# Block order of the second and third count products in a four-layer graph network on one Trainium2 core

## The reference, cut to what matters

```python
deg_inv_sqrt = jnp.where(deg > 0, jax.lax.rsqrt(jnp.maximum(deg, 1.0)), 0.0)
w = deg_inv_sqrt[src] * deg_inv_sqrt[dst]
x = emb
out = emb
for _ in range(NUM_LAYERS):              # 3
    x = jax.ops.segment_sum(w[:, None] * x[src], dst, num_segments=n)
    out = out + x
return out / (NUM_LAYERS + 1)
```

## Time and profile before

| | |
|---|---|
| median of 3 runs | 1010.4 us (1008.99 to 1014.34) |
| the profiled execution's own time | 1007.57 us |
| its span in the trace | 1005.9 us |
| TensorE matmul busy | 840.9 us (84%), 14240 instructions |
| VectorE busy | 856.4 us (85%), 1214 instructions |
| ScalarE busy | 616.1 us (61%) |
| GpSimd busy | 192.8 us (19%) |
| mean granted TensorE clock | 0.94 |

### The profile page before, as it was taken

The page is one execution under the profiler, slowest core; times in us unless marked ns, Lnnn a source line. Parts: engine busy times, 40 slices in busy tenths (PEclk is TensorE's granted clock), DMA queues, the critical chain, the costliest instruction groups (busy, mean ns, idle before and its releaser), DMA issues. The chain is left out here.

```text
span 1005.9 us, 33666 instructions
## 1 busy us (share of the span) xinstructions
PE 840.9 (84%) x14240; PEld 589.8 (59%) x14240; DVE 856.4 (85%) x1214; ACT 616.1 (61%) x2090; POOL 192.8 (19%) x364
## 2 busy tenths in 40 slices
PE   0596549998888988898889988639999998999996
PEld 0362435555555554555555555329999998885653
DVE  8987879999999998999999999466666895786995
ACT  0763448788777887787777877359999902111000
POOL 4823832223222321223222322000000000000000
PEclk9879559999999999999999999959999999997999
DMA  9942316766766676657775777599100001964993
GB/s 205 224 158 77 64 49 142 176 149 172 172 168 151 169 170 156 166 136 181 173 176 135 184 168 178 135 368 414 43 2 2 2 1 49 367 241 168 344 398 103
DMA packets 44698, 164.33 MB, mean 163 GB/s; under 512 B 14244, under 2 KB 16374, under 8 KB 40822
## 3 DMA queue, kind: packets, MB, share of 16 engines
q1 hardware_dynamic: 33990, 133.22, 43.3%
q0 software_dynamic: 8288, 27.59, 13.3%
q10 hardware_dynamic: 2256, 1.23, 0.5%
HBM read 78.63 MB, written 63.72 MB: 142 GB/s over the span
## 5 line engine op out<-in xcount | busy, mean ns | idle before, releaser
L1187 PEld LDWEIGHTS b_ps<-b_mv,b_soh 64*128 64x128 bf16 x9600 | 162.3, 95 | 133.8 <-DVE b_mv L1069 64.7
L1187 PE MATMUL b_ps<-b_mv,b_soh 64*128 64x50 bf16 (+1 forms) x9600 | 186.7, 189 | 63.2 <-DVE b_mv L1069 36.0
L1417 PE MATMUL layers_ps<-layers_u,layers_c 128*128 128x192 bf16 x2500 | 211.8, 248 | 10.3 <-ACT layers_u L1599 7.7
L1417 PEld LDWEIGHTS layers_ps<-layers_u,layers_c 128*128 128x128 bf16 x2500 | 208.7, 99 | 15.6 <-DVE layers_y L1723 8.0
L957 ACT ACTIVATE b_c_row<-b_ps 128x300 bf16<-128x300 f32 (+1 forms) x275 | 116.9, 425 | 55.3 <-PE b_ps L1187 51.8
L1069 DVE TENSOR_TENSOR b_mv<-b_mv,b_parts 128x2808 bf16<-128x2808 bf16 x100 | 145.9, 1459 | 1.6
L977 ACT ACTIVATE b_pos<-b_ps,k_coef 128x1024 f32<-128x1024 f32 x100 | 92.8, 928 | 63.1 <-PE b_ps L1187 58.3
L1608 ACT ACTIVATE k_passed<-layers_c 128x128 bf16<-128x128 bf16 x450 | 131.4, 293 | 0.0
L1107 DVE TENSOR_TENSOR b_y<-b_sim,b_ps 128x512 f32<-128x512 f32 (+1 forms) x175 | 109.6, 627 | 19.4 <-PE b_ps L1244 12.3
L1064 DVE TENSOR_TENSOR b_soh<-k_numbers,b_bits 128x2304 bf16<-128x2304 bf16 x100 | 122.3, 1223 | 0.0
L1096 DVE SCALAR_TENSOR_TENSOR b_sim<-b_ps,k_coef,b_pos 128x1024 f32<-128x1024 f32 x100 | 104.5, 1045 | 7.7 <-ACT b_pos L977 7.7
(11 more groups left out here) (275 smaller groups left out, 1091.5 us busy)
## 6 DMA issues: line engine op xcount, KB each, us to landing
layers_c<-g_blocks SPq DMA_DIRECT2D x25, 1600.0 KB, 9.1
g_blocks<-b_g_row SPq DMA_DIRECT2D x52, 400.0 KB
c_blocks<-b_c_row SPq DMA_DIRECT2D x25, 800.0 KB
g_blocks<-head_odd SPq DMA_DIRECT2D x48, 400.0 KB
layers_c<-c_blocks SPq DMA_DIRECT2D x12, 1600.0 KB, 26.4
k_passed<-b_sent POOLq DMA_DIRECT2D x24, 768.0 KB, 7.0
prep_attr<-in_edge_attr SPq DMA_DIRECT2D x2, 1883.0 KB
prep_attr<-in_edge_attr SPq DMA_DIRECT2D x1, 1876.0 KB
```

The lines of the kernel that those rows point to most:

```text
L1187: return nc.tensor.matmul(out, lhsT, rhs, start=start, stop=True, skip_group_check=True)
L1417: return nc.tensor.matmul(out_, lhsT, rhs, start=start, stop=True, skip_group_check=True)
```

## The change

`LATE = 20` is new. In the products 1 and 2 the first four pairs run over the source blocks 0 to 19, pair after pair, and then over the source blocks 20 to 24, pair after pair; the pairs 4 to 12 run as before. Product 0, product 3 and all other engines' instructions are as they were.

```diff
+LATE = 20
...
             def narrow():
-                for layer in range(3):
-                    for g in range(NP2):
+                for g in range(NP2):
+                    product(0, g, 0, NB)
+                for layer in range(1, 3):
+                    for h0, h1 in ((0, LATE), (LATE, NB)):
+                        for g in range(4):
+                            product(layer, g, h0, h1)
+                    for g in range(4, NP2):
                         product(layer, g, 0, NB)
                 for g in range(4):
                     product(3, g, *HALVES[0])
```

## The result

The changed kernel took 1021.63 us, the median of 17 runs (1015.8 to 1028.0). The kernel before, run beside it, took 1013.16 us, the median of 17 (1008.99 to 1017.75). The ratio is 1.0083, with a 95% interval of 1.0059 to 1.0107, so the change costs 8.5 us by the medians and 6.0 to 10.8 us by the interval. The prediction had said slower, by 0.69%, and 1017.4 us with a range of 1014.2 to 1021.3 us. The direction holds, and the forecast change of 7.0 us lies within the interval; the time itself lies 0.3 us above the range.

What follows compares the result with a forecast made beforehand. Product 1 was taken as bound by TensorE, product 2 by VectorE. 9.90 - 1.47 - 1.47 + 0 = +6.96 us on a 1010.4 us median gave 1017.4 us, 0.69% slower, range 1014.2 to 1021.3 us.

Steps and rivals of the forecast that it cites:

- The transitions: TensorE's waits for VectorE's last `split` on entering products 1 and 2: both go, 1.47 us each.
- VectorE's lag: In product 1 VectorE starts late, 5.1 us behind, wins 1.24 us per pair and catches up at pair 8 or 9.
- the term that decides: Product 2: VectorE's first sum waits for 120 more matmuls, +9.90 us less two transition waits, +6.96 us, nothing given back.
- The 51.15 us from there to product 3: Distance from product 2's first sum to product 3's first matmul, said to stay as it was; another value would be wrong.
- Short waits of TensorE in product 2: Pairs 7 to 11 each wait some 0.96 us for VectorE's sums, at no cost, being covered by VectorE's work.
- the rival in which the clock falls in product 2: Short pauses put TensorE at half level from pair 6 on: 13.2 us more, 1030.6 us; chance 0.04.
- The clock at product 3's start: Loss to the half clock after TensorE's 8.7 us pause: 1.6 in place of 1.7 us, change taken as 0.
- The rival that the start is absorbed: VectorE makes up its late start in product 2, so only the transitions count: 1007.5 us, not slower; chance 0.06.
- the last step: From the profiled execution's 1014.5 us to a median: 2.8 us above the profiled 1007.57, so 1010.4 + 7.0 = 1017.4 us.
- part of the scatter: Allowance for run scatter in the range: 1.5 us at the lower end, 2.2 us at the upper.

Runs made afterwards that it cites:

- e1: New order in product 1 only, product 2 in the old order, against the kernel before: ratio 1.000 (0.997 to 1.003).
- e4: Changed kernel with three VectorE counts moved ahead of product 2's first sum, the other four after its pairs 0 to 3; against the kernel before: ratio 0.9935.
- e2: New order in product 2 only, product 1 in the old order, against the kernel before: ratio 1.0099 (1.0069 to 1.0130).
- e7: The changed kernel run once more, nothing else altered, against the kernel before: ratio 1.0074 (1.0044 to 1.0105).
- e5: Changed kernel with three counts ahead of product 1's first sum, three ahead of product 2's, the last after its pair 0; against the kernel before: ratio 0.9915.
- e8: The kernel before run once more as a measure of scatter, against the kernel before: ratio 0.9995 (0.9963 to 1.0027).
- e6: Kernel before in its old order, only counts moved: four into product 1, three after pairs 0, 2, 4 of product 2; against the kernel before: ratio 0.9931.
- e3: New order for the first two pairs instead of four, in both products, against the kernel before: ratio 1.0006 (0.9966 to 1.0045).

## Why the prediction was right, and where it was wrong

*The transitions.* Both waits went, at 1.47 us each: e1 has 1.46 for one of them. The records of TensorE show them as 1.28, and it was right to read the price from the distance of sums instead.

*Product 1.* VectorE's lag was forecast to be gone at pair 8 or 9, and it is gone at pair 9.

*Product 2, the term that decides.* +9.90 us for 120 matmuls less 2.94 gives +6.96 us; the trace has +6.99. The 51.15 us from there to product 3 didn't change. That VectorE's queue is in order, so that the counts stand behind the waiting sum, was argued in the prediction; e4 shows it.

*Short waits of TensorE in product 2.* Forecast: 0.96 us for each of five pairs, at no cost. The trace has five of 0.79 or 0.80 us in its records (0.96 less what the last record overlaps), and e2's loss, which has the same five, is explained without them. The clock stayed at full level. So the rival in which the clock falls in product 2 is out, by five pauses of 0.8 us with 1.00 granted around each. The rule of the Trainium skill, "TensorE: Matmul & The Clock Gate", section "A second HAM failure mode: psum-queue depth-cycling", that small idle times between matmul groups can make the clock go up and down, does not show at pauses of this size.

*The clock at product 3's start* was taken as 0 between -1.7 and +1.7 us. It measured +0.40 (14.36 against 13.96 us from first matmul to first sum), and 0.46 in e7.

*The rival that the start is absorbed* fell, and for the reason given: e4 shows that it holds once there is work without a dependency.

*What failed* is the last step, "the median of the runs shown is 2.8 us above it, and gives 1010.4 + 7.0", with its "part of the scatter", 2.2 us, at the upper end. The median of 3 runs stood for the level of the kernel before. Beside the changed kernel that level was 1013.16 us, 2.8 us higher; beside e1 to e4 it was 1008.58 and beside e5 to e8 1015.13 us. The same kernel's level thus moves by 6.6 us from set to set, nearly as much as the change itself. It goes with the granted clock: the medians of the executions' mean clocks were 0.941 beside e1 to e4 and 0.935 beside e5 to e8. 1013.16 x 1.0069 would have been 1020.2 us. The remaining 1.5 us (8.5 by the medians, 7.0 forecast) lie within the interval of the ratio, and what they are made of is open; the 0.40 us of clock at product 3's start don't explain them, since 0.39 us come back behind it. The profiled execution shows the same failure larger: 1014.5 us was forecast for it and it took 1023.35, of which 8.44 us are the later start of product 0 and 0.36 us the slower first sum. The term to size otherwise was the scatter of the level, some 3 us to either side, and it stood in the range with 1.5 and 2.2 us.

## What to carry to other kernels

Ask of each reordering who owns the chain behind it. Finishing several accumulations together lets the producer go past one late input, but delays the consumer's first piece by all that was put ahead of it; that is free where the consumer has idle time later (product 1) and costs its full length where it has none (product 2). Before such a change, look in the consumer's in-order queue for work that depends on nothing, and move it into the wait: the same order that lost 0.8% gains with the counts moved. Most of that gain is the moved counts' and not the order's: e6 has 4.54 us of e5's 8.47 with the old order, and the order adds 2.9. And read a small change from the distance of two events in its own stage, since the total of this kernel scatters by as much as the change (1008.99 to 1017.75 us before).

## What the runs showed of the hardware that was not expected

Instructions that no experiment touched took 673.50 us up to product 0 in one execution and 686.75 us in another. The difference grows through the build stage, and it goes with the granted clock there. Between 170 and 640 us TensorE had a mean clock of 1.00 in the kernel before and of 0.99 in e1, e2, e3 and e8, which all began product 0 by 677.72 us; it had 0.98 in the changed kernel, e5, e6 and e7 and 0.97 in e4, which began it at 681.53 us or later. The stretches of the kernel before and of the changed one (length, busy, granted clock, DMA share, GB/s):

```profile
170.00:640.00 470.00, 416.38 (x10041) 1.00 0.68 164
...
170.00:640.00 470.00, 417.49 (x10047) 0.98 0.68 163
```

One such fall can be followed from row to row. The same two instructions of VectorE, with TensorE's stretch from 283 to 287 us set between them, first in the kernel before and then in the changed one:

```profile
280.10 0.68 DVE L1107 TENSOR_TENSOR b_y<-b_sim,b_ps 128x512 f32<-128x512 f32 x1
283.00:287.00 4.00, 4.00 (x89) 1.00 0.02 4
285.58 0.69 DVE L1107 TENSOR_TENSOR b_y<-b_sim,b_ps 128x512 f32<-128x512 f32 x1
...
282.07 0.68 DVE L1107 TENSOR_TENSOR b_y<-b_sim,b_ps 128x512 f32<-128x512 f32 x1
283.00:287.00 4.00, 3.34 (x68) 0.52 0.40 93
290.22 0.69 DVE L1107 TENSOR_TENSOR b_y<-b_sim,b_ps 128x512 f32<-128x512 f32 x1 [1.77 <-PE b_ps L1244]
```

They are 5.48 us apart in the one and 8.15 us in the other. The whole executions agree: of the 35 of the kernel before beside e1 to e4, the eight with a mean clock of 0.937 or less had a median of 1015.3 us, and the 18 above 0.940 one of 1006.4 us. Why the clock falls in one execution and not in another is open.

The time at the half clock at product 0's start differs for the same instructions. The first sum came 5.90 us after the first matmul in one trace and 7.06 us in another (e3), where at full level it would be 4.33 us. So that start cost between 1.6 and 2.7 us, and a comparison of single executions carries it.
